# Two expert FFNs around a Mamba block: gated rows scattered into the residual with an accumulating transfer

## What is computed

```python
x = x + 0.5 * moe_ffn(layernorm(x))     # 8 experts, each token uses its 2 best
x = x + mamba2(layernorm(x))            # projection, conv, scan over time, gate, projection
x = x + 0.5 * moe_ffn(layernorm(x))     # the same weights again

def moe_ffn(x):
    logits = x @ router_w.T
    top_vals, top_idx = top_k(logits, 2)
    top_w = softmax(top_vals)            # the gates
    y = square(relu(x @ w1[e])) @ w2[e]  # for every expert e; 256 -> 512 -> 256
    return sum over k of top_w[:, k] * y[top_idx[:, k]]
```

## Time and profile before

| what | value |
|---|---|
| runs, median (lowest to highest) | 1262.8 us (1258.38 to 1271.11) |
| profiled execution, span | 1265.8 us |
| busy PE, weight load | 1050.3 us (83%), 870.1 us (69%) |
| busy DVE, ACT, POOL | 748.1, 605.8, 607.9 us (59%, 48%, 48%) |
| DMA moved | 112.20 MB, mean 89 GB/s |
| first FFN, loading and routing; tile loop | 0 to about 110; about 110 to 371 us |
| Mamba | about 375 to 927 us |
| second FFN, routing; tile loop; end | 927 to 965; 965 to 1226; 1226 to 1266 us |

### The profile page before, as it was taken

How to read it: one execution, slowest core, us unless ns; L and a number is a source line. 1 busy time by engine, 2 the same in 40 slices (tenths; PEclk the granted TensorE clock), 3 DMA queues, 4 the chain that set the end, 5 groups by cost and what they waited for, 6 DMA issues and landing times. The chain is left out here.

```text
span 1265.8 us, 21732 instructions
## 1 busy us (share of the span) xinstructions
PE 1050.3 (83%) x6532; PEld 870.1 (69%) x6532; DVE 748.1 (59%) x1614; ACT 605.8 (48%) x1560; POOL 607.9 (48%) x612
## 2 busy tenths in 40 slices
PE   3746999999965788989898888989836999999960
PEld 2745999999954556666676666657525999999950
DVE  5974444444427778677878786865355444444437
ACT  1323555555533455556555656565314555555530
POOL 6922555555531245354545454647502555555520
PEclk9997999999985598899989989999858999999985
DMA  7872222322313101111111110000061232222339
GB/s 227 276 294 74 76 76 76 99 76 76 76 59 93 38 30 43 42 42 42 43 42 42 43 38 17 27 17 21 22 279 38 88 97 92 94 95 91 100 117 327
DMA packets 73258, 112.20 MB, mean 89 GB/s; under 512 B 10680, under 2 KB 60352, under 8 KB 71872
## 3 DMA queue, kind: packets, MB, share of 16 engines
q1 hardware_dynamic: 48704, 60.48, 14.2%
q0 software_dynamic: 13824, 37.77, 9.3%
q10 hardware_dynamic: 10624, 12.58, 2.9%
HBM read 66.76 MB, written 44.04 MB: 88 GB/s over the span
## 5 line engine op out<-in xcount | busy, mean ns | idle before, releaser
L427 POOL DMA_INDIRECT ys_d<-xs,row_of x144 | 142.4, 989 | 195.6 <-DVE xs L811 188.2
L422 POOL DMA_INDIRECT xs<-xn_d,token_of x144 | 140.1, 973 | 115.1 <-DVE token_of L785 71.8
L491 ACT ACTIVATE hs<-pH 128x512 f32<-128x512 f32 x144 | 86.0, 597 | 227.6 <-PE pH L613 217.6
L800 DVE TENSOR_TENSOR xl<-pT,xh 128x256 fp32r<-128x256 f32 x144 | 61.1, 424 | 212.7 <-PE pH L613 108.7
L805 DVE TENSOR_TENSOR h2l<-hs,h2h 128x512 fp32r<-128x512 f32 x144 | 99.8, 693 | 81.3 <-ACT h2h L499 77.3
L1604 DVE SCALAR_TENSOR_TENSOR acc<-bank,cwh,acc 128x511 f32<-128x511 f32 (+2 forms) x120 | 89.6, 747 | 40.5 <-ACT acc L1218 37.7
L633 PE MATMUL pY<-w2h,h2h 128*128 x576 | 103.5, 302 | 1.4 <-DVE h2l L805 1.2
L1122 POOL TENSOR_TENSOR yv<-yv,sz 128x512 f32<-128x512 f32 x32 | 40.7, 1272 | 120.6 <-DVE yv L1643 117.4
L613 PE MATMUL pH<-w1h,xh 128*128 x288 | 93.0, 405 | 1.8 <-DVE xl L800 1.1
L613 PE MATMUL pH<-w1l,xh 128*128 x288 | 92.3, 402 | 0.0
L633 PE MATMUL pY<-w2h,h2l 128*128 x576 | 91.1, 280 | 0.0
(11 more groups left out here) (250 smaller groups left out, 2591.4 us busy)
## 6 DMA issues: line engine op xcount, KB each, us to landing
m_yg<-ys_d SPq DMA_DIRECT2D x64, 128.0 KB, 2.1
xs<-ys_d SPq DMA_DIRECT2D x12, 512.0 KB, 6.8
wst<-in_L_ffn_w_dram ACTq DMA_DIRECT2D x8, 512.0 KB, 4.6
xs<-in_L_attn_x_dram SPq DMA_DIRECT2D x8, 512.0 KB, 6.5
hs<-in_L_ffn_w_dram ACTq DMA_DIRECT2D x8, 512.0 KB, 4.7
xn_d<-xs SPq DMA_DIRECT2D x8, 512.0 KB, 3.4
lo_d<-w1l SPq DMA_DIRECT2D x1, 4096.0 KB, 11.8
lo_d<-w2l SPq DMA_DIRECT2D x1, 4096.0 KB, 21.4
```

The source lines that it names most:

```text
L422: pool.indirect_dma_start(out=xg[:, t % NX, :], out_offset=None, in_=xn_d, in_offset=bass.IndirectOffsetOnAxis(ap=token_of[:, t:t + 1], ax ...
L427: pool.indirect_dma_start(out=ys_d, out_offset=bass.IndirectOffsetOnAxis(ap=row_of[:, t:t + 1], axis=0), in_=y[:, t % NX, :], in_offset=No ...
L491: act.activation(r[:, u, :], pH[u][:, :], ACT.Relu).then_inc(relu_done.sem, 1)
```

## The change

Each FFN adds its gated rows into the residual in DRAM: the first into `x1_d`, a copy of x that SP makes DRAM to DRAM during routing; the second into `x2_d`. `ys_d` is gone. The scatter is an accumulating transfer (`compute_op=ALU.add`), and `row_of` is now the token, so a row receives two scatters; POOL therefore waits, ahead of scatter t, until scatter t-1 has landed. Empty slots go to 128 spare rows behind the residual.

The gate must be applied before the scatter. `xn_d` gets two more columns (DG = D + 2): the first gate, and the second minus the first. ACT writes them for all tokens in one transfer of 8 bytes a row, before the first gather, which waits for it (`gates_stored`); DVE works the gates out ahead of piece 2 instead of behind the pieces. A gather brings 258 columns; `pick_gate` (one DVE operation of 128x1 a tile) selects the gate, and `copy_y` multiplies by it.

The Mamba block loads one tensor, `x1_d`, instead of three; the two additions are gone. At the end, the second FFN copies `x2_d` to `out` DRAM to DRAM in two transfers of 2 MB. The loads of `res` and of `ys_d`, the 64 additions and the 8 stores are gone. The spill, which stood ahead of the wait for `experts_known` in SP's program, now stands behind it, with the early weights behind the spill as before, but with no wait for the spill's landing between.

```diff
-            xg, y = xs[:, 0:NX, :], xs[:, NX:2 * NX, :]
+            xg = xs[:, 0:NX * DG].rearrange("p (n d) -> p n d", d=DG)
+            y = xs[:, NX * DG:NX * (DG + D)].rearrange("p (n d) -> p n d", d=D)
...
@@ sync, first FFN
+                sp.dma_start(acc_d[0:TOK, :], x).then_inc(base_stored, 16)
                 sp.wait_ge(w_lo.sem, w_lo.done(NW - 1))
+                sp.wait_ge(experts_known, 1)
                 sp.dma_start(lo_d[0], w1l[:, :].bitcast(F32)).then_inc(w_spilt, 16)
                 sp.dma_start(lo_d[1], w2l[:, :].bitcast(F32)).then_inc(w_spilt, 16)
-                sp.wait_ge(w_spilt, 32)
-                sp.wait_ge(experts_known, 1)
                 sp.dma_start(early["wo"][:, :, :], early["w_out"].rearrange("(k p) n -> p k n", p=P)).then_inc(out_loaded, 16)
...
@@ sync, second FFN
-                for n in range(T // EG):
-                    sp.wait_ge(y_copied.sem, y_copied.done(n * NT // (T // EG)))
-                    sp.dma_start(res[:, n * EG:(n + 1) * EG, :], tiles(x, n * EG * P)).then_inc(res_loaded, 16)
                 for u in range(NX):
                     sp.wait_ge(scattered[u].sem, scattered[u].done(NT // NX - 1))
-                for n in range(T // EG):
-                    if n >= NE:
-                        sp.wait_ge(e_done.sem, e_done.done((n - NE + 1) * EG - 1))
-                    for k in range(TOP):
-                        sp.dma_start(er[n % NE][:, k, :, :], tiles(ys_d, n * EG * P + (1 + k * T) * P)).then_inc(e_loaded[n % NE].sem, 16)
+                for n in range(2):
+                    part = slice(n * TOK // 2, (n + 1) * TOK // 2)
+                    sp.dma_start(out[part, :], acc_d[part, :]).then_inc(out_stored, 16)
+                sp.wait_ge(out_stored, 2 * 16)
...
@@ gpsimd
             pool.wait_ge(routed, 1)
+            pool.wait_ge(gates_stored, 16)
...
                 if t >= NX:
                     pool.wait_ge(g_T.sem, g_T.done(t - NX))
+                    pool.wait_ge(gate_known.sem, gate_known.done(t - NX))
...
                 pool.wait_ge(y_copied.sem, y_copied.done(t))
-                pool.indirect_dma_start(out=ys_d, out_offset=bass.IndirectOffsetOnAxis(ap=row_of[:, t:t + 1], axis=0),
-                                        in_=y[:, t % NX, :], in_offset=None).then_inc(scattered[t % NX].sem, 16)
+                if t > 0:
+                    pool.wait_ge(scattered[(t - 1) % NX].sem, scattered[(t - 1) % NX].done((t - 1) // NX))
+                pool.indirect_dma_start(out=acc_d, out_offset=bass.IndirectOffsetOnAxis(ap=row_of[:, t:t + 1], axis=0),
+                                        in_=y[:, t % NX, :], in_offset=None, compute_op=ALU.add).then_inc(scattered[t % NX].sem, 16)
...
@@ scalar
+                if piece == 3:
+                    act.wait_ge(gates_known, 1)
+                    act.dma_start(xn_d.rearrange("(t p) d -> p t d", p=P)[:, :, D:DG], gates[:, :, :]).then_inc(gates_stored, 16)
...
@@ vector
+                if piece == 2:
+                    weigh()
...
-                dve.tensor_copy(y[:, t % NX, :], pY[t % 2][:, 0:D]).then_inc(y_copied.sem, 1)
+                dve.wait_ge(gate_known.sem, gate_known.done(t))
+                dve.tensor_scalar(y[:, t % NX, :], pY[t % 2][:, 0:D], gate[:, t:t + 1], None, ALU.mult).then_inc(y_copied.sem, 1)
+
+            def pick_gate(t):
+                dve.wait_ge(gathered[t % NX].sem, gathered[t % NX].done(t // NX))
+                dve.scalar_tensor_tensor(gate[:, t:t + 1], xg[:, t % NX, D + 1:DG], second[:, t:t + 1], xg[:, t % NX, D:D + 1],
+                                         ALU.mult, ALU.add).then_inc(gate_known.sem, 1)
...
@@ Mamba, sync and vector
-                for r in range(TOP):
-                    sp.dma_start(yg[:, i % 2, r, :], ys_d[(i + 1 + r * T) * P:(i + 2 + r * T) * P, :]).then_inc(y_loaded[i % 2].sem, 16)
...
-                dve.scalar_tensor_tensor(a, yg[:, i % 2, 0, :], gates[:, i:i + 1], a, ALU.mult, ALU.add).then_inc(add1.sem, 1)
...
-                dve.scalar_tensor_tensor(a, yg[:, i % 2, 1, :], gates[:, i + T:i + T + 1], a, ALU.mult, ALU.add).then_inc(add2.sem, 1)
```

More of the change, by code:

```diff
@@ L163, in _, with ffn_block @@
                                               base=0, pattern=[[sign, P]], channel_multiplier=-sign))
-def ffn_block(nc, c, keep, x, router_w, w1, w2, xn_d, ys_d, lo_d, out, first, tables=None, early=None):
-    TOK = x.shape[0]
+def ffn_block(nc, c, keep, x, router_w, w1, w2, xn_d, acc_d, lo_d, out, first, tables=None, early=None):
+    TOK = xn_d.shape[0]
     T = TOK // P
@@ L211, in ffn_block @@
         rwT, logits = keep["rwT"], keep["logits"]
-        scratch = Carved(tables if first else sb("room" + tag, [P, T * D], F32))
-        res = None if first else scratch.tensor[:, :].rearrange("p (i d) -> p i d", d=D)
+        scratch = Carved(tables if first else sb("room" + tag, [P, 4 * WORDS], F32))
         iota_e = scratch.take([T, E], F32)
@@ L237, in ffn_block @@
         spare = sb("spare" + tag, [P, NT], F32)
+        second = sb("second" + tag, [P, NT], F32)
+        gate = sb("gate" + tag, [P, NT], F32)
         row_of = sb("row_of" + tag, [P, NT], U32)
@@ L279, in ffn_block @@
             step(n) for n in ("g_T", "g_hi", "g_split", "h_ready", "relu_done", "rT_ready", "sq_done", "h2_split", "y_ready", "y_copied"))
-        e_loaded = [step(f"e_loaded{u}", 16 * TOP) for u in range(NE)]
+        gate_known = step("gate_known")
         out_loaded, early_loaded, early_hi, early_split = (sem(n) for n in ("out_loaded", "early_loaded", "early_hi", "early_split"))
-        res_loaded, e_stored = sem("res_loaded"), sem("e_stored")
-        e_first, e_done = step("e_first"), step("e_done")
+        gates_known, gates_stored, base_stored, out_stored = (sem(n) for n in ("gates_known", "gates_stored", "base_stored", "out_stored"))
         def across(ap, n):
@@ L432, in _ @@
             pool.wait_ge(routed, 2)
+            if first:
+                pool.wait_ge(base_stored, 16)
             for t in range(NT):
@@ L528, in _ @@
                     square(t + 1, (t + 1) % 2)
[L529 to L533, removed]
         @block.tensor
@@ L662, in _ @@
         def _(dve):
-            for s in (w_hi, st_chain, mv_done, var_done, norm_done, oh_hi, oh_lo, g_split, h2_split, y_copied):
+            for s in (w_hi, st_chain, mv_done, var_done, norm_done, oh_hi, oh_lo, g_split, h2_split, y_copied, gate_known):
                 s.open(dve)
@@ L761, in _, with weigh @@
             link(dve.tensor_copy(parts_b[:, :, :], parts_i[:, :, :]))
+            def weigh():
+                dve.wait_ge(exp_out, 1)
+                link(dve.tensor_scalar(top[:, 4, :], top[:, 3, :], 1.0, None, ALU.add))
+                link(dve.reciprocal(top[:, 5, :], top[:, 4, :]))
+                link(dve.tensor_scalar(gates[:, :, 0], top[:, 5, :], 0.5, None, ALU.mult))
+                link(dve.tensor_tensor(top[:, 4, :], gates[:, :, 0], top[:, 3, :], ALU.mult))
+                dve.tensor_tensor(gates[:, :, 1], top[:, 4, :], gates[:, :, 0], ALU.subtract).then_inc(gates_known, 1)
             for piece in range(C // PC):
                 at, u = slice(piece * PC, (piece + 1) * PC), piece % 2
+                if piece == 2:
+                    weigh()
                 if piece >= 2:
@@ L787, in _ @@
             link(dve.scalar_tensor_tensor(row_f[:, 2, :], row_f[:, 0, :], 0.0, spare[:, :], ALU.is_equal, ALU.mult))
-            dve.tensor_tensor(row_of[:, :], row_f[:, 0, :], row_f[:, 2, :], ALU.add).then_inc(routed, 1)
+            dve.wait_ge(routed, 1)
+            dve.tensor_tensor(row_of[:, :], token_of[:, :], row_f[:, 2, :], ALU.add).then_inc(routed, 1)
+            link(dve.tensor_scalar(second[:, :], row_f[:, 0, :], float(TOK + P), None, ALU.is_ge))
             upto = small[:, 2, :].rearrange("p (a e) -> p a e", a=1).to_broadcast([P, NT, E])
@@ L837, in _ @@
                 copy_y(t)
[L840 to L852, removed]
+                if t + 2 < NT:
+                    pick_gate(t + 2)
 def make_keep(nc, ctx, tokens):
@@ L862, in make_keep @@
         "w2h": sb("w2h", [P, E * WCOLS], F32R),
-        "gates": sb("gates", [P, TOP * tokens // P], F32),
+        "gates": sb("gates", [P, tokens // P, DG - D], F32),
         "logits": sb("logits", [P, tokens // P, E], F32),
@@ L898, in early_weights, with mamba_block @@
             "w_in": w_in, "w_out": w_out, "norm_w": norm_w}
[L901 to L903 removed]
+def mamba_block(nc, c, keep, early, x, conv_w, conv_b, dt_bias, a_log, d_skip, x2, xn_d, batches):
+    TOK = xn_d.shape[0]
     T = TOK // P
@@ L917, in mamba_block @@
         ident, tri = c["ident"], c["incl_tri"]
-        gates, logits, rwT = keep["gates"], keep["logits"], keep["rwT"]
+        logits, rwT = keep["logits"], keep["rwT"]
         wih, wil, wo = early["wih"], early["wil"], early["wo"]
@@ L929, in mamba_block @@
         xr = sb("xr", [P, RX, D])
-        yg = sb("m_yg", [P, 2, TOP, D])
         st, st2 = sb("m_st", [P, 6]), sb("m_st2", [P, 6])
```

(5 more changed lines are left out.)

58 lines of the change are left out of this document (19 added, 39 removed).

## The result

The changed kernel takes 1426.9 us (median of 4 runs, 1420.5 to 1431.5) beside 1265.2 us for the kernel before: a ratio of 1.125 [1.120, 1.131]. Forecast were 1242 us, with a range of 1226 to 1333. It is slower by 162 us, far outside. A kernel can run in a slower state now and then, and medians and ratios leave such runs out: two of six of the last kernel of experiment eight.

What follows compares the result with a forecast made beforehand. PE was taken to bound the FFN loops, PE and DVE Mamba, DVE and DMA the tail. Terms -17.6 + 6.5 + 2 - 8 - 4 = -21 us gave 1244.7 from the profiled 1265.8, 1242 as median; range 1226 to 1333.

Steps and rivals of the forecast that it cites:

- The scatter chain: Both FFN loops: POOL waits for each scatter to land; 3.2 us a cycle, hidden under the tiles' 3.42, loop cost nothing.
- rival (1): Both FFN loops: POOL's wait for scatter t-1 becomes the bound, slower than before above a 3.60 us cycle; chance 0.33.
- C: POOL's cycle in the FFN loops: an adding scatter's landing time plus the step to POOL's next start; 3.2 us taken.
- The choice between the ends: POOL's cycle, bounds 2.65 and 4.45 us: 3.2 taken, since source and old content can be fetched side by side.
- the case that was forecast: Both FFN loops: scatter waits hidden, sum as predicted; 1242 us, own range 1228 to 1256, chance 0.45.
- Tail: End of the second FFN: 39.4 us replaced by a 21.8 us DRAM to DRAM copy, gain 17.6 us (10.9 to 27.6).
- Rival (2): Final copy at half the spills' rate, 43.6 us: no change, 1264 us; chance 0.17, shared with cycles of 3.5 to 3.69.
- Spill beside the first gathers: Start of the first FFN: the later spill slows the first gathers and two scatters, +2 us (0 to +6).
- Ends of the FFNs: Last scatters of each FFN, where tiles come faster and the wait is not covered: +3.2 us, twice, +6.5.
- Gates: Before each FFN's first gather: earlier DVE gate work and ACT's transfer of 4,096 pairs hidden, 0, up to +3.5 per FFN.
- Mamba: Mamba stage, fewer loads and no DVE additions: -8 us in the lead-in (-3 to -10), -4 in steady slots (0 to -20).
- rival (3): Mamba stage bound by DVE: all 22 slots give 0.91 us, -20 instead of -4, 1226 us; chance 0.05.

Runs made afterwards that it cites:

- the last kernel of experiment eight: Changed kernel with POOL's scatters waiting only where the expert changes, and the spill put ahead of the wait for experts_known: 1238.5 us, ratio 0.978 to the kernel before.
- experiment eight: Changed kernel, but a scatter waits for the one before only where the expert changes, SP releasing POOL: 1243.8 us, ratio 0.982 to the kernel before.
- Experiment one: Changed kernel with plain instead of adding scatters, the wait for the previous scatter kept (sums not formed): 1248.6 us, ratio 0.983 to the kernel before.
- experiments six: Changed kernel with only the spill put back ahead of the wait for experts_known: 1421.0 us, 5.9 us less than the changed kernel.

## Why the prediction was wrong, by its own steps

**The scatter chain is the step that failed.** The mechanism was named, as rival (1), with a chance of 0.33: wait for scatter t-1, price 2 x 71 x (C - 3.42). With the measured medians, 4.59 and 4.60, that is 167 of the 188.6 us by which the loops grew; the rest are the longer steps. PE starves, as in that case, though by the other route that the prediction named: its gathers are late, not its `y` buffers. What failed is the size of C: 3.2 us was taken, 4.45 stood as the upper bound, 4.6 is the median. It has three parts, and the value taken was too small in each:

| part of C | taken, us | upper bound, us | measured, us |
|---|---|---|---|
| POOL's issue | 0.97, as for a plain scatter | 0.97 | 1.59 |
| landing beyond the issue | 1.95: the plain one's 1.40 and 0.55 for adding | 3.2: 1.40 and a gather's 1.8 | 2.25 |
| landing to POOL's next start | 0.28, read off a copy on DVE | 0.28 | 0.75 |
| sum | 3.2 | 4.45 | 4.59 |

Of the 1.39 us that were missing, 0.62 are the issue, 0.47 the step to the next start and 0.30 the landing. The first and third parts were held fixed in both bounds, so the upper bound was none: it priced one part of three. "More descriptors for POOL" stood among the grounds for rival (1), without a price. The third could have been doubted from the rows at hand. 0.28 us is the step from a DVE operation to POOL; none of the rows read had POOL start a scatter behind a landing, so that part had no row of its own. With 0.75 in its place the value taken becomes 3.67 and the upper bound 4.92: the first already past the 3.60 at which rival (1) decides.

The choice between the ends ("nearer to the plain scatter than to two trips") was not what failed. The measured 2.25 is nearer to 1.40 than to 3.2, if only just, and with the other two parts as taken it would have given C = 3.50, under 3.60. The prediction also concluded that the chain can't be loosened; experiment eight loosens it at all but eight steps of each FFN.

**The two figures of the Trainium skill's page "DMA: Bandwidth & Descriptors", section "Latency and other measured facts".** The estimate from 0.2 us for an HBM access was C 2.85, that from 2 us at high load 4.65. The measured 4.6 is beside the second, and so is the time that it gave, 1,412 us beside 1,427. But the makeup is not that one: of the 1.94 us by which 4.59 exceeds 2.65, 0.62 are POOL's issue, 0.85 the landing beyond it and 0.47 the step. The agreement is not evidence for a 2 us access.

**The rest of the sum came out near, in part by luck.** Experiment one is the case that was forecast: its cycle is 3.16 to 3.19 us where 3.2 was supposed, and it takes 1248.6 us where 1242 were forecast, with 1228 to 1256 as that case's own range. But errors cancel in it. In the profiled executions its loops took 21.2 us more than those of the kernel before, where 6.5 were taken; the stretch between the loops took 18.8 less and the tail 23.5 less, where 12 and 17.6 were taken.

- *Tail.* -17.6 was taken. From the last landing (1406.03 + 3.7) to the end are 16.4 us where there were 39.4: -23.0, of which 1.3 goes back into the longer landing. SP issues the copy 3.74 us after the last scatter's start, and the 4.19 MB have landed 15.0 us later, 1.3 us before the end:

```profile
1406.03 1.55 POOL L426 DMA_INDIRECT x_d<-xs,row_of  x1 [2.88 <-DMA x_d<-xs,row_of]
1409.77 1.14 SPq L378 DMA_DIRECT2D out_dram<-x_d  x2
```

  That is between the bounds (11.8 and 28.5); the two spills, taken as its price at 21.8, were no likeness of it. Rival (2), a copy at half the spills' rate, is out.
- *Spill beside the first gathers.* +2 taken; the first scatter comes 4.0 us late, and the step to the second is 5.3 us longer than without the spill, which the sum did not have at all.
- *Ends of the FFNs.* Part of the chain now, as rival (1) said.
- *Gates.* 0, as forecast. The transfer of the 4,096 pairs lands 8.8 and 7.9 us after its issue (4.5 were taken, 17 was the bound): issued at 91.87 and 1040.81, ahead of the first gathers at 107.16 and 1056.84. Beside the spill it came to 16.7 and 18.0 (experiments six and eight), and there the first gather waited for it.

```profile
xs<-xn_d,token_of POOLq DMA_INDIRECT x144, 2.9
x_d<-xs,row_of POOLq DMA_INDIRECT x144, 3.8
...
xn_d<-gates ACTq DMA_DIRECT2D x2, 32.0 KB, 8.4
out_dram<-x_d SPq DMA_DIRECT2D x2, 11.7
```

- *Mamba.* -12 taken; the stretch from the first FFN's last scatter to the second's first, which holds the Mamba stage, is 10.6 us shorter. Its DVE time fell to 403.5 us, from 424.8. The size is not settled: kernels with the same code there but for row offsets took 590 to 604 us for this stretch, at granted clocks of 0.90 to 0.88, where the kernel before had 0.87. So the gain lies between 10 and 23 us, the larger figures go with the higher clocks, and rival (3) is neither shown nor out.

In experiment eight, where the chain is out of the way and nothing else of the change is missing, the total comes out as forecast: a ratio of 0.982, where 1242 / 1262.8 = 0.984 was forecast. In its profiled execution the start and the loops took 4.6 us more than before, the stretch between them 9.7 less and the tail 22.5 less.

## What to carry to other kernels

A transfer that must wait for the one before takes its whole round trip at every step, and that is hidden only while the rest of the step is longer (3.2 us beside 3.42 in experiment one, 4.6 no more): the issue on its engine, the landing beyond it, and the step from a landing back to the next start. Take each of the three from a row of its own kind, and where there is no such row widen the bound for that part too. Then ask where two transfers can really meet: ordering at 8 steps per FFN instead of 71 turned 12.5% slower into 1.8% faster.

## What the runs showed of the hardware that I had not expected

- Adding makes the indirect scatter longer in two places: 128 rows of 1 KB take POOL 1.59 us to issue instead of 0.99, with the wait or without, and land 3.8 us after the start instead of 2.4. It goes out in 128 packets of 1 KB, the plain one in 32 of 4 KB; an adding packet of 1 KB takes 102 ns in the median, one of SP's queue 46.
- POOL started a scatter 0.7 us after its queue had taken the wait, whether the landing itself or SP released it, and 0.28 us after a copy on DVE. Why is open.
- 4.19 MB went from DRAM to DRAM in 15.0 us, in two transfers, 8.4 MB read and written; the two spills of the kernel before wrote 8.4 MB in 21.8 us.
- 4,096 pieces of 8 bytes landed in 6.5 to 8.8 us, and in 16.7 to 18.0 beside the spill.
